# Attention plus routed experts on one core: another order of the steps between attention and the experts, and of the sums in the back end

## What is computed

```python
x = x + xattn(layernorm(x), ctx, ctx, pad_mask, subsq_mask, Wq, bq, Wk, bk, Wv, bv)   # 16 heads of 16
xf = layernorm(x)
ys = geglu(xf @ Ws1 + bs1) @ Ws2 + bs2                  # the shared expert, 512 wide
top_val, top_idx = top_k((xf @ Wr + br) / 1.5, 2)       # the router
w = one_hot(top_idx) weighted by softmax(top_val)
h = einsum('nd,edh->enh', xf, We1) + be1                # 12 experts, 768 wide
yr = einsum('end,ne->nd', einsum('enh,ehd->end', geglu(h), We2) + be2, w)
x = x + ys + yr
```

## Time and profile before

| what | us |
|---|---|
| median of 3 runs (lowest, highest) | 647.09 (646.93, 648.26) |
| the profiled execution's own time | 648.26 |
| its span, first to last instruction | 646.4 |
| TensorE busy (share of the span) | 599.0 (93%) |
| VectorE busy | 462.3 (72%) |
| ScalarE busy | 302.1 (47%) |
| GpSimd busy | 348.9 (54%) |

### The profile page before, as it was taken

How to read it: one execution, slowest core, us unless ns; L and a number is a source line. 1 busy time by engine, 2 the same in 40 slices (tenths; PEclk the granted TensorE clock), 3 DMA queues, 4 the chain that set the end, 5 groups by cost and what they waited for, 6 DMA issues and landing times.

```text
span 646.4 us, 14884 instructions
## 1 busy us (share of the span) xinstructions
PE 599.0 (93%) x4422; PEld 501.8 (78%) x4423; DVE 462.3 (72%) x1037; ACT 302.1 (47%) x677; POOL 348.9 (54%) x403
## 2 busy tenths in 40 slices
PE   8789999998987995799999999999999999999995
PEld 6678777876865885678887888878887888889995
DVE  6879878888968476766666666666676776665767
ACT  4456666666654334234444444444444444444432
POOL 3791001101079568777883985778986683000773
PEclk9989999999998799999999999999999999999998
DMA  8937661563813343426444355263455230000443
GB/s 280 346 109 284 230 224 72 191 244 142 301 66 125 110 150 133 146 91 228 133 138 169 121 199 183 81 228 131 154 210 184 84 130 32 32 29 22 138 133 122
DMA packets 47910, 98.95 MB, mean 153 GB/s; under 512 B 4736, under 2 KB 23808, under 8 KB 47872
## 3 DMA queue, kind: packets, MB, share of 16 engines
q1 hardware_dynamic: 36192, 50.40, 22.3%
q0 software_dynamic: 10976, 47.72, 21.7%
q10 hardware_dynamic: 704, 0.33, 0.2%
HBM read 57.15 MB, written 39.19 MB: 149 GB/s over the span
## 4 chain that ended last, share of the span: by engine, by line
PE 73%; DVE 13%; ACT 5%; issue 5%; POOL 2%; DMA 1%; DVEq 0%; SPq 0%; ACTq 0%; POOLq 0%
PE ps_s L789 27%; PE ps_o L822 10%; PE ps_s L751 6%; PE ps_o L823 5%; PE ps_t L586 4%; PE ps_t L799 3%; PE ps_t L515 2%; PE ps_s L574 2%; PE ps_x L515 2%; PE ps_s L569 2%; DVE nmax L1323 2%; PE ps_o L596 1%; PE ps_s L799 1%; PE ps_x L810 1%; DVE xn L1229 1%
## 5 line engine op out<-in xcount | busy, mean ns | idle before, releaser
L789 PE MATMUL ps_s<-ring,xTh 128*128 x516 | 152.6, 417 | 0.0
L1798 POOL TENSOR_TENSOR ring<-stage,ring 128x512 fp32r<-128x512 f32 x80 | 100.9, 1295 | 1.2
L789 PEld LDWEIGHTS ps_s<-ring,xTh 128*128 128x128 f32 x516 | 89.0, 190 | 14.9 <-issue 0.7
L822 PE MATMUL ps_o<-ring,hTh 128*128 x258 | 97.0, 413 | 3.7 <-DVE hTl L1621 3.7
L1612 DVE TENSOR_TENSOR ag<-ps_s,up_bias 128x512 f32<-128x512 f32 x129 | 88.7, 687 | 12.9 <-PE ps_s L789 10.7
L789 PE MATMUL ps_s<-ring,xTl 128*128 x258 | 80.5, 393 | 0.0
L1786 POOL TENSOR_TENSOR ve<-mv,eps 128x2 f32<-128x2 f32 x16 | 4.0, 247 | 133.0 <-DVE mv L1355 119.0
L823 PE MATMUL ps_o<-ring,hTl 128*128 x258 | 72.7, 282 | 0.0
L1103 ACT ACTIVATE ps_s<-ag 128x256 f32<-128x256 f32 x129 | 50.2, 389 | 42.8 <-DVE ag L1612 41.9
L1978 POOL DMA_INDIRECT gath<-rows_out,idx_out x32 | 31.0, 969 | 66.3 <-DMA rows_out<-y_row 56.9
L1617 DVE TENSOR_TENSOR ag<-ag,ps_s 128x256 f32<-128x256 f32 x129 | 54.3, 421 | 16.1 <-ACT ps_s L1103 0.5
(11 more groups left out here) (272 smaller groups left out, 1346.4 us busy)
## 6 DMA issues: line engine op xcount, KB each, us to landing
rows_in<-y_row SPq DMA_DIRECT2D x8, 3328.0 KB, 12.6
stage<-in_w POOLq DMA_DIRECT2D x12, 1536.0 KB, 6.8
stage<-in_w POOLq DMA_DIRECT2D x12, 768.0 KB, 5.4
up_bias<-in_bias POOLq DMA_DIRECT2D x12, 768.0 KB, 4.5
xrow<-rows_in SPq DMA_DIRECT2D x43, 128.0 KB, 2.5
rows_out<-y_row SPq DMA_DIRECT2D x43, 128.0 KB, 1.7
cbuf<-in_ctx SPq DMA_DIRECT2D x8, 256.0 KB, 2.9
xn_all<-xn2p SPq DMA_DIRECT2D x8, 256.0 KB, 2.3
```

Source lines behind the costliest of these rows:

```text
L789: last = pe_.matmul(ps_s[:, i, :], x[:, c, :], weights(place, off + c * 2 * HR + i * 2 * D, 2 * D), start=n == 0, stop=n == 5)
L822: pe_.matmul(ps_o[:, :], hTh[i][:, c, :], weights(place, a, 2 * D), start=i == 0 and c == 0, stop=False)
L1798: last = pool.tensor_tensor(lo_ap[:, c:c + PIECE], src[:, c:c + PIECE], hi_ap[:, c:c + PIECE].bitcast(f32), ALU.subtract)
```

## The change

The steps keep their arithmetic; what changes is where they stand in each engine's queue.

- The last pair's small steps are "r", "n", "l" instead of "r", "l", "n", and all engines issue them inside `pair` rather than behind it. VectorE does `choose(1,1)` ahead of `norm` of batch 14, and `row_numbers(1)` behind the three steps.
- Behind the pairs, TensorE does `x_group(0)` behind the first prob-transposes of batch 15, a single filler matmul (`spin`), and `chunk_ups(0,0)` to `(0,2)` each one place further ahead of that batch's `values` and `out_transposes`.
- GpSimd issues the scatters of tiles 3 to 6 at the start of pair 7 and that of tile 7 behind its `rstd`, then `first_w1`; `convert_down` of the first W2 goes behind the last `rstd`, ahead of the scatters of tiles 8 to 15.
- In front and back, `chunk_down(g-1, 3)` is one `chunk_ups` earlier, `sums(g-1)` is earlier on VectorE, and the combines behind chunks 0 and 1 are one chunk earlier.

```diff
         if last:
-            return ["r", "l", "n"]
+            return ["r", "n", "l"]
...
                 values(0, par, prev)
                 if tail:
                     put("cT", again=first)
-                if not last:
-                    put("r")
+                put("r")
                 out_transposes(prev)
+                if last:
+                    put("n")
                 if tail:
                     put("xT", again=first)
-                if not last:
-                    put("l")
+                put("l")
...
             prob_transposes(B - 1, 0)
-            router("r", PAIRS - 2, LAST_R, LAST_R % 2)
+            pe.wait_ge(xb_free, PAIR_STEPS_END - 1)
+            x_group(0)
             prob_transposes(B - 1, 1)
-            router("l", PAIRS - 2, LAST_R + 1, (LAST_R + 1) % 2, LAST_R + 1)
-            prob_transposes(B - 1, 2)
-            pe.wait_ge(xb_free, LAST_R + 2)
-            x_group(0)
-            prob_transposes(B - 1, 3)
             pe.wait_ge(converted, 1)
             pe.wait_ge(shifted, UNITS)
+            spin(SPIN, ps_s[:, 3, 0:D])
+            prob_transposes(B - 1, 2)
             chunk_ups(0, 0, SH)
+            prob_transposes(B - 1, 3)
+            chunk_ups(0, 1, SH)
             values(1, 1, B - 1)
-            chunk_ups(0, 1, SH)
+            chunk_ups(0, 2, SH)
             out_transposes(B - 1)
-            chunk_ups(0, 2, SH)
-            rank_step(LAST_R + 2, LAST_R % 2, 1)
             chunk_ups(0, 3, SH)
...
                 chunk_ups(g, 0, SH)
+                chunk_down(g - 1, 3, SH)
                 chunk_ups(g, 1, SH)
-                chunk_down(g - 1, 3, SH)
...
                 if last:
                     ln2_apply(p - 1)
+                    choose(1, 1)
                 norm(p, 0)
...
-                if not last:
-                    put("l")
+                if last:
+                    put("n")
+                put("l")
+                if last:
+                    ve.wait_ge(xb_free, index_of("n", p, first, last) + 1)
+                    row_numbers(1)
...
                     chunk_gate(g, 0)
+                    sums(g - 1)
                     hidden_low(g, 0)
+                    combine_behind(g, 0)
                     chunk_gate(g, 1)
-                    sums(g - 1)
                     hidden_low(g, 1)
-                    combine_behind(g, 0)
+                    combine_behind(g, 1)
                     chunk_gate(g, 2)
                     hidden_low(g, 2)
-                    combine_behind(g, 1)
...
                 if last:
-                    gp.wait_ge(xb_free, base_of(p, first))
-                    first_w1()
+                    paced_scatters(range(3, 7), (p * 2 - 1) * 4)
...
+                if last:
+                    paced_scatters((7,), p * 8)
+                    gp.wait_ge(xb_free, base_of(p, first))
+                    first_w1()
...
             each_pair(gp, pair)
-            gp.wait_ge(scores_ready, B)
-            gp.wait_ge(raw2_in, 16)
-            convert_down(stage2[:, :], ring[:, 0, 2 * W1R:], 4).then_inc(converted, 1)
-            gp.wait_ge(converted, 2)
-            load_raw2(1)
-            paced_scatters(range(3, 7), (B - 1) * 4)
             rstd(ln2_var, ln2_rs, mv2, ve2, rs2, PAIRS - 1, pstep2)
-            scatter(7)
...
+            gp.wait_ge(scores_ready, B)
+            gp.wait_ge(raw2_in, 16)
+            convert_down(stage2[:, :], ring[:, 0, 2 * W1R:], 4).then_inc(converted, 1)
+            gp.wait_ge(converted, 2)
+            load_raw2(1)
             gp.wait_ge(xn2_saved, 16 * 6)
```

20 lines of the change are left out of this document (6 added, 14 removed).

## The result

The change makes the kernel slower. The median goes from 647.11 to 656.5 us (655.94 to 657.1 over the runs), a ratio of 1.0142 with a 95% interval of 1.0124 to 1.016. The profiled execution took 655.67 us with a span of 653.8, against 648.26 and 646.4 before. The direction was forecast, the size not: +3.1 us expected, +9.4 measured on the medians, +7.4 between the two profiled executions. The range's upper end of 653 was passed.

A forecast was written before the change was run, and what follows sets the result against it. TensorE, busy in 93% of the span, was taken as the bound, with movable time at the attention-to-experts handover and back end. +3.0 +1.7 -1.6 = +3.1 gave 650.2 us; own range 648.6 to 651.8, 8 in 10 from 643.5 to 653.

The forecast's parts named there:

- (1): Attention's end: with `first_w1` off `choose(0,1)`, `xn2p` takes 1.1 us and the router's transposes start 3.2 us earlier.
- (2): `choose(1,1)` beside `first_w1`: small operations are held, `chosen` ready at 207.6 (bounds 205.7 and 210), and TensorE's clock falls.
- rival (C): Heavier: each small operation waits a whole TENSOR_TENSOR, `chosen` at 210, `chunk_ups` at 218, 652.7 us in all; chance 0.1.
- (3): Start of the shared experts: `chunk_ups(0,0)`, released by `xgl`, starts at 215.5 against 214.06, +1.4 us.
- (4): Up to the last residual: added TensorE work, less the earlier clock return, adds +1.6, so out-transposes end +3.0 us.
- (5): GpSimd's queue: `convert_down` ahead of scatters 8 to 11 costs +2.9, partly taken up by scatter 12's wait: +1.7 us.
- (6): Front group 2: earlier `sums(1)` removes a TensorE wait, but the first row tile hangs on the scatters: 0.
- (7): Back end: three waits for `x_all` go (1.1 us) and `combine(11)` moves (0.5): -1.6 us, bounds -2.1 and 0.
- (A): Rival: small operations slip between GpSimd's instructions, clock stays full, `chunk_ups(0,0)` 3.9 us earlier, 642.7 us in all; chance 0.22.

The follow-up runs named there:

- e12: The change with only the six TENSOR_TENSORs of `first_w1` waiting for `chosen`, its TENSOR_SCALARs staying on `xn2p`: 647.97 us, ratio 1.0015 to the kernel before.
- e3: The change with GpSimd starting `first_w1` only when `chosen` of batch 1 is ready: 643.98 us, ratio 0.9973 to the kernel before.
- e1: The change with TensorE's old order in the back groups (`chunk_down(g-1,3)` behind `chunk_ups(g,1)`): 655.92 us, ratio 1.013 to the kernel before.
- e4: The change with `convert_down` of the first W2 and its load moved ahead of `rstd(7)`: 654.62 us, ratio 1.011 to the kernel before.
- e9: The kernel of e3 run again (the change, `first_w1` behind `chosen`): 645.09 us, ratio 0.998 to the kernel before.
- e11: The kernel of e9 with the W2 load issued behind the last scatter and `combine` behind `hidden_low(g,3)`: 645.23 us, ratio 0.9981 to the kernel before.
- e17: The kernel of e10 with the change's edits of the back groups and `combine` moved: 644.36 us, ratio 0.9962 to the kernel before.
- e10: The kernel before with the change's GpSimd program and `first_w1` behind `xn2p`, other engines in old order: 644.94 us, ratio 0.9975 to the kernel before.
- e15: The kernel of e3 with `combine` moved and five idle matmuls ahead of `chunk_down(0,0)`, on a disturbed chip: ratio 1.0074 to the kernel before.

## Why the prediction was right in sign and too small

**(1) `choose(0,1)` freed, the transposes of `xn2p` earlier: right, half the size.** The `eq` of `choose(0,1)` took 0.21 and `xn2p` started right behind `values(14)`, as forecast. But it took 2.69 us, not the 1.1 taken and above the bound of 1.9. The bound assumed that each of its two instructions waits at most one TENSOR_SCALAR of 0.59. The first of the two took 2.08 us (200.96 to 203.04), across the ends of four of them. e12 shows that the TENSOR_SCALARs alone do it (2.59). The transposes came 2.86 behind `values(14)` instead of the 1.5 forecast, 1.8 us earlier than before instead of 3.2.

**(2) The step that failed: how long `choose(1,1)` is held.** The place and the mechanism were named; the term for the holds was mis-sized. The forecast had 3.8 us from `xn2p` to `chosen` ("three or four of them at half a microsecond or so"). It was 7.4. All six operations named were held, by 0.91, 0.99, 0.74, 0.98, 0.79 and 1.14 us, in sum 5.55 on top of the undisturbed 1.9. Each waits for nearly the whole TENSOR_TENSOR of 1.23 us (7.38/6), since it comes right behind one that has just been let through; the ends given above show it. That goes for `ex` with its four elements a partition and for the cast, which has one input. The one `eq` pair in the earlier trace rows, +0.76 and +0.98, showed this price; I took three or four holds of half a microsecond, 1.9 in all, a third of what came. I also let part of the chain fall beside TENSOR_SCALARs, which `xn2p`, itself held, used up. So `chosen` came 10.1 behind `values(14)`, forecast 5.2, rival (C) 7.6. Rival (C) had the right mechanism, but it charged the six holds with 4.3 us in all, 0.7 each, and not with the whole TENSOR_TENSOR that it names. e3 removes the holds and the loss with them. In e1 and e4, with the same front, five were held and `chosen` came at 9.0.

The Trainium skill's rule (page SBUF — State Buffer, section "Who interferes with whom") says more than I used. It also says that a reduction never contends on this chip. The trace agrees: `best` took 0.20 in the midst of the held ones. `xn2p` at 2.69 beside TENSOR_SCALARs and the held cast fit what it says of one-input operations in a two-port mode, though the trace doesn't show the mode. Had I charged each of the six operations with a whole TENSOR_TENSOR of 1.27, the chain would have come out at 7.6 us, against 7.4 measured.

**(3) The first `chunk_ups`: +1.4 forecast, +5.0 measured.** `chosen` came 4.9 later than forecast, 1.3 by the longer `xn2p` and 3.6 by the held chain, and this step gave 1.3 back. It was not released by `xgl`: nothing held `x_all` or `row_numbers(1)`, since `first_w1` had ended (the 4 us taken for that were 0). TensorE did ranks, router, transposes and a filler at half clock without a gap and was itself what ended last.

**(4) Up to the last residual: +1.6 forecast, 0 measured.** The out-transposes of batch 15 moved by 5.05, as much as the first `chunk_ups`. The 2.3 us of added work were given back in full, because the clock was back 1.2 us behind the first `chunk_ups` (a mean of 0.62 over 215 to 220 puts it at 218.8), where before it was 5.3. The rule of the step (later start, less of it at half clock) was right and was applied with the too small shift. `chunk_down(0,0)` and `rstd(7)` moved by the same 5.05, as forecast.

**(5) GpSimd's queue: +1.7 forecast, +3.0 measured.** From the end of `rstd(7)` to scatter 8 it was 7.65 against 4.19 us: +3.5, forecast +2.9. The 1.24 us ahead of scatter 12 were not used up, 0.95 stayed, because `idx_top` of the last batch came later too, by 8.4 us: it, and not the queue, ended last there. TensorE's clock was at half from 229 to 239. This second fall was in none of my cases, and it is what made `idx_top` so late: from `chunk_down(0,0)` to the last `idx_top` it is 18.2 us in the change, e1 and e9, with the fall, and 15.3 in e3 and e4, without it. It stands right behind a wait of 2.03 us for `hTl` ahead of `chunk_down(0,0)`, 0.38 before. That wait is not a hold: e3 and e4 have the same 2.03, in e3 with an `hTl` of 0.42. It is the `chunk_ups` drawn forward over the out-transposes, which I costed at nothing: it had covered VectorE's norm, residual and gate. `chunk_down(0,0)` itself is no later for it. What `convert_down` alone costs is not shown: e4 takes it away, and its time doesn't stand clear of the change's.

**(6) `sums(1)`: 0, as forecast**; nothing in the profiles speaks against it.

**(7) Back end: -1.6 forecast, +0.45 measured (57.26 against 56.8).** The three waits for `x_all` did go, and `combine(11)` left its place (the last wait for `hTl` fell from 1.10 to 0.15 and 0.36). What I did not ask is what `chunk_down(g-1,3)` needs when it comes one `chunk_ups` earlier: `hTl` of chunk 3, which stood behind a `combine` of 1.0 us. Three waits of 0.65 to 0.70 took the place. e11 and e17 show it by moving that `combine`: these three waits are gone, and the back end falls to 55.5 and 55.7. This step missed by 2.05 us, the second largest error of the sum.

**The rivals.** (A) is refuted by the change and shown possible by e3: with no conversion on the choice, `chunk_ups(0,0)` came 3.5 earlier than before, close to the 3.9 that (A) gave (its own terms, 205.7 + 1.1 + 2.5, add up to 209.3 and not to 210.2). But e10 gets 4.3 with the old order, so the new order is not what wins there. The chance of 0.22 for it was too high for what stood in GpSimd's queue, and the 0.1 for (C) too low. Sum of the steps as measured from `values(14)` on: +5.0, 0, +3.0 and +0.85 behind the tile (0.45 of it in the back end), so +8.9, close to the +9.4 of the medians. Of the 5.8 that the forecast lacked, 3.6 stand at the first `chunk_ups`, -1.6 in step 4, 1.3 in step 5, 2.05 in step 7 and 0.4 between the first tile and the back end. That the error of step 4 pays for that of step 5 is luck.

What stays open: why the clock falls a second time in some executions of one kernel and not in others. e3 and e9 are the same kernel, with times from 642.6 to 650.1. Both waited 2.03 us for `hTl` ahead of `chunk_down(0,0)`; e9's clock then fell (0.66 over 220 to 235) and e3's did not (1.00), while e3's had fallen earlier (0.84 over 205 to 215). The long wait isn't needed for the fall: e10 and e17, with the old order, waited 1.01 and 0.98 us there and fell as well (in e10 0.67 over 220 to 225 and 0.65 over 225 to 230). e15 was meant to tell and ran on a chip that hid it.
